# A fused attention and expert kernel: x transposed by its transfer, and the first block in another order

## What is computed

```python
x = x + layernorm(attention(layernorm(x)))
x = x + layernorm(experts(layernorm(x)))

# attention(y): 8 heads of 32, linear, chunks of 64
q, k, v = y @ Wq.T, y @ Wk.T, y @ Wv.T
o = q @ (running sum of k.T @ v) + masked(q @ k.T) @ v
denom = maximum(abs(sum(q * cumsum(k))), 1.0)
o = rmsnorm(o / denom, norm_w) @ Wo
# experts(y): 8 experts of 256, all of them on every row, weighted by a router
out = sum_e w_e * ((silu(y @ Wg[e]) * (y @ Wu[e])) @ Wd[e])
```

## Time and profile before

| | |
|---|---|
| median of 3 runs | 1476.51 us (1476.43 to 1479.62) |
| the profiled execution | 1476.86 us, of which the span 1475.1 us |
| PE, DVE, ACT, POOL busy | 98%, 68%, 43%, 29% of the span |
| from block to block | 89.2 us (transposes of x from 66.8 to 1315.3 us, 14 blocks) |

### The profile page before, as it was taken

How to read it: one execution, slowest core, us unless ns; L and a number is a source line. 1 busy time by engine, 2 the same in 40 slices (tenths; PEclk the granted TensorE clock), 3 DMA queues, 4 the chain that set the end, 5 groups by cost and what they waited for, 6 DMA issues and landing times. The chain is left out here.

```text
span 1475.1 us, 36709 instructions
## 1 busy us (share of the span) xinstructions
PE 1450.9 (98%) x14182; PEld 1263.7 (86%) x14182; DVE 1000.3 (68%) x2397; ACT 629.5 (43%) x1159; POOL 425.6 (29%) x621
## 2 busy tenths in 40 slices
PE   7899999999999999999999999999999999999997
PEld 6688888888888888888888888888888888888886
DVE  6757667586675767667585675767667676675765
ACT  5434534444353443534445353443534345344432
POOL 2402424123241223414134241232413134241230
PEclk9999999999999999999999999999999999999999
DMA  5100000000000000000000000000000000000000
GB/s 173 58 2 16 15 0 14 14 14 14 0 27 1 14 14 14 14 0 14 14 14 14 0 14 14 14 14 0 28 0 14 14 14 14 0 15 16 1 8 22
DMA packets 25344, 24.58 MB, mean 17 GB/s; under 512 B 2016, under 2 KB 25056, under 8 KB 25312
## 3 DMA queue, kind: packets, MB, share of 16 engines
q1 hardware_dynamic: 25312, 24.13, 5.2%
HBM read 15.74 MB, written 8.39 MB: 16 GB/s over the span
## 5 line engine op out<-in xcount | busy, mean ns | idle before, releaser
L1057 DVE TENSOR_TENSOR late<-late,up_ps 128x512 f32<-128x512 f32 x256 | 175.0, 683 | 145.6 <-PE up_ps L455 113.5
L825 ACT ACTIVATE late<-gate_ps 128x512 f32<-128x512 f32 x256 | 152.6, 596 | 278.0 <-PE gate_ps L455 277.2
L455 PE MATMUL down_ps<-w_hi,h_hi 128*128 128x256 f32 x976 | 264.7, 293 | 0.0
L735 ACT ACTIVATE h_hi<-late 128x512 fp32r<-128x512 f32 x256 | 161.2, 630 | 225.1 <-DVE late L1057 225.0
L455 PE MATMUL down_ps<-w_hi,h_lo 128*128 128x256 f32 x976 | 254.2, 282 | 0.0
L1291 POOL TENSOR_TENSOR rms_in<-rms_in,minus_half 128x16 f32<-128x16 f32 x32 | 93.4, 2918 | 489.5 <-DVE rms_in L1005 489.5
L1079 DVE SCALAR_TENSOR_TENSOR late<-down_ps,route,late 128x256 f32<-128x256 f32 x364 | 158.5, 477 | 86.8 <-PE down_ps L455 84.2
L937 DVE TENSOR_TENSOR h_lo<-late,h_hi 128x512 fp32r<-128x512 f32 x256 | 175.6, 686 | 61.0 <-ACT h_hi L735 61.0
L455 PE MATMUL gate_ps<-ft_hi,w_hi 128*128 128x512 f32 x512 | 204.3, 399 | 1.2 <-ACT ft_hi L735 0.8
L455 PE MATMUL gate_ps<-ft_hi,w_lo 128*128 128x512 f32 x512 | 203.0, 397 | 0.0
L455 PE MATMUL up_ps<-ft_hi,w_hi 128*128 128x512 f32 x512 | 199.7, 390 | 0.0
(11 more groups left out here) (175 smaller groups left out, 2381.7 us busy)
## 6 DMA issues: line engine op xcount, KB each, us to landing
xs<-in_x SPq DMA_DIRECT2D x32, 256.0 KB, 2.8
out_rows<-late SPq DMA_DIRECT2D x32, 256.0 KB, 2.2
late<-in_wg SPq DMA_DIRECT2D x7, 256.0 KB, 2.7
late<-in_wu SPq DMA_DIRECT2D x7, 256.0 KB, 4.4
late<-in_wd SPq DMA_DIRECT2D x6, 256.0 KB, 4.1
late<-in_wkv_t SPq DMA_DIRECT2D x1, 512.0 KB, 4.0
x<-in_wd SPq DMA_DIRECT2D x2, 256.0 KB, 5.6
late<-in_wq_t SPq DMA_DIRECT2D x1, 256.0 KB, 4.7
```

The source lines that it names most:

```text
L455: last = nc.tensor.matmul(dst, lhs, rhs, start=n == 0, stop=n == len(terms + low_terms) - 1)
L735: return nc.scalar.activation(dst, src, ACT.Copy)
L825: nc.scalar.activation(h_f[:, m, :], gate_ps[:, :], ACT.Silu).then_inc(silu_ready[0], 1)
L1057: nc.vector.tensor_tensor(h_f[:, m, :], h_f[:, m, :], up_ps[m][:, :], ALU.mult).then_inc(h_ready[0], 1)
```

## The change

First, x transposed. From block 1 on PE no longer transposes. The raw x comes a second time by transfer, element by element, into `x_t`, the free half of `kz`: eight transfers of 128x128 elements a block. SP issues those of block i+1 when block i has split its own, and those of block 1 when the scores of block 0 are done; there they stand behind all weight units. ACT and DVE split `x_t`. The mean is taken out by centred weights: at the start PE forms the column means of the q, k and v weights with a matrix of 1/256 in `rz`, and DVE subtracts them before they are split. The inverse deviation comes in where ACT copies k and v out of PSUM, tile by tile, as a scale; q stays unscaled, and the bound of the denominator is multiplied by x's variance instead, which POOL writes to `var_s` and four small transfers (`place_var`) bring into the layout of the heads (`var_o`). `normalise_x` goes.

Second, block 0. Its PE transposes now go into banks of their own order, its steps stand in another order on all four engines, with other counts of warm-up products, and `x_stats` of block 1 stands behind the first expert's hidden steps on DVE, `x_root` behind `routing` on POOL.

The diff, cut:

```diff
+FIRST_PE = [("xt", 0), ("xt", 1), ("kv", 0), ("kv", 1), ("q", 0), ("su", 0), ("kt", 0), ("su", 1), ("q", 1), ("kt", 1),
+            ("s", 0), ("s", 1), ("o", 0), ("o", 1), ("ot", 0), ("ot", 1), ("wo", 0), ("wo", 1), ("ft", 0), ("ft", 1)]
...
+FIRST_WARM = {("kv", 0): 3, ("kt", 0): 1, ("su", 1): 2, ("s", 1): 1, ("ot", 0): 16, ("ot", 1): 8, ("ft", 0): 27, ("ft", 1): 3}
...
+        x_t = kz[:, :, :, 1, :]
...
+            def load_x_t(row):
+                for t in range(TILES):
+                    p, b = divmod(t, B)
+                    for k in range(KT):
+                        sp.dma_start(x_t[:, k, p, b * P:b * P + P],
+                                     x[b, bass.ds(row + p * P, P), k * P:k * P + P].rearrange("c n -> n c"),
+                                     allow_slow_non_contiguous=True).then_inc(xt_loaded[0], 16)
+
+
+            def place_var(block):
+                reach(sp, var_ready, block, 0)
+                for g in range(HG):
+                    for i in range(2):
+                        sp.dma_start(var_o[C * g:C * g + C, :, i], var_s[C * i:C * i + C, :], allow_slow_non_contiguous=True).then_inc(var_loaded[0], 16)
...
+            reach(sp, att_done, (0, 0), number_of(("s", 1), (0, 0)) + 1)
+            load_x_t(ROWS)
             reach(sp, x1_ready, (0, 0), 2)
             load_x(ROWS)
+            place_var((1, 0))
             with sp.Fori(1, BLOCKS - 1) as i:
+                reach(sp, xt_ready, (i, 0), KT)
+                load_x_t(i * ROWS + ROWS)
                 reach(sp, x1_ready, (i, 0), 2)
                 load_x(i * ROWS + ROWS)
+                place_var((i, 1))
                 store_out((i, -1), i * ROWS - ROWS)
...
-                    else:
-                        k = step[1]
-                        reach(pe, xn_ready, a, TILES)
-                        for t in range(TILES):
-                            last = nc.tensor.transpose(dst[:, t // 2, t % 2 * P:t % 2 * P + P],
-                                                       rows[:, t, k * P:k * P + P], ident[:, :])
...
+            warm(6)
+            for n, (raw, loaded, columns) in enumerate(((wkv_raw, att_w_loaded[1], 2 * HID), (wq_raw, att_w_loaded[0], HID))):
+                pe.wait_ge(loaded, 16)
+                for k in range(KT):
+                    last = nc.tensor.matmul(up_ps[n][:, 0:columns], rz, raw[:, k, :], start=k == 0, stop=k == KT - 1)
+                last.then_inc(mean_done, 1)
...
+                elif kind == "xt":
+                    reach(act, xt_loaded, a, 0)
+                    copy(halves(xt_hi[:, step[1], :]), x_t[:, step[1], :, :]).then_inc(xt_hi_ready[0], 1)
...
+                elif kind == "kv" and not is_first(a):
+
+                    reach(act, rstd_ready[0], a, 2)
+                    for b in range(B):
+                        t = 2 * step[1] + b
+                        last = nc.scalar.activation(k_sb[:, t, :], src[:, b, 0:HID], ACT.Copy, scale=rstd1[:, t:t + 1])
...
-                if more:
-                    normalise_x((a[0], a[1] + 1))
...
+                    else:
+
+                        reach(dve, var_loaded, a, 0)
+                        den_sq, bounded = (flat.rearrange("p b (i j) -> p (b i) j", i=2) for flat in (o_sq[:, :, :, D], den2[:, :, :]))
+                        nc.vector.scalar_tensor_tensor(bounded, den_sq, RMS_EPS,
+                                                       var_o[:, 2 * p:2 * p + 2, :].rearrange("p b i -> p (b i)").unsqueeze(2)
+                                                       .broadcast_to([P, 2 * B, HPG]), ALU.mult, ALU.max)
...
-            x_stats((1, 0))
             low_of_unit(UNITS - 2)
             low_of_unit(UNITS - 1)
             for m in range(MT):
                 hidden(0, m, (0, 0))
                 low_hidden(0, m, (0, 0))
+            x_stats((1, 0))
             first_expert((1, 0), (0, 0), None)
```

More of the change, by code:

```diff
@@ L85 @@
 ]
[L88 to L99, removed]
-             ("ln3_stats", 0), ("ln2_stats", 1), ("unit", 18), ("ln2_add", 1), ("ln3_stats", 1), ("ln3_norm", 0), ("unit", 19),
-             ("ln3_norm", 1), ("ft_out", 0), ("ft_out", 1), ("unit", 20), ("unit", 21)]
@@ L291, in build_program @@
         READ_OUT = {ROUTER: (rz_copied, 1), ROUTER_T: (tanh_ready, 1)}
-        for n in range(KT):
-            READ_OUT["xt", n] = (xt_ready, n + 1)
         for n in range(HG):
@@ L495, in att_step @@
             def att_step(step, a):
+                if step[0] == "xt" and is_first(a):
+                    p = step[1]
+                    pe.wait_ge(xn_ready[0], 2 * p + 2)
+                    for k in range(KT):
+                        for t in range(2):
+                            last = nc.tensor.transpose(att_ps[:, 2 * p + k, t * P:t * P + P], rows[:, 2 * p + t, k * P:k * P + P],
+                                                       ident[:, :])
+                    last.then_inc(xt_done, 1)
                 if step not in PSUM_STEPS:
@@ L704, in _ @@
                 att_step(step, (0, 0))
+            warm(3)
             pe.wait_ge(w_ready, ATT_W + 3)
@@ L743, in ln_apply @@
                 return last
-            def normalise_x(a):
-                for t in range(TILES):
-                    ln_apply(1, 2, a, rows, xs, [t], shift1, rstd1).then_inc(xn_ready[0], 1)
             def normalise_out(p, f):
@@ L757, in att_step @@
                 half = slice(2 * P * step[1], 2 * P * step[1] + 2 * P) if len(step) > 1 else None
-                if kind == "xt":
-                    copy(xt_hi[:, :, half] if is_first(a) else halves(xt_hi[:, step[1], :]), src).then_inc(xt_hi_ready[0], 1)
+                if kind == "xt" and is_first(a):
+                    act.wait_ge(xt_done, step[1] + 1)
+                    copy(xt_hi[:, :, half], att_ps[:, 2 * step[1]:2 * step[1] + 2, 0:2 * P]).then_inc(xt_hi_ready[0], 1)
+                elif kind == "xt":
+                    reach(act, xt_loaded, a, 0)
+                    copy(halves(xt_hi[:, step[1], :]), x_t[:, step[1], :, :]).then_inc(xt_hi_ready[0], 1)
                 elif kind == "q":
                     copy(q_t[:, :, half] if is_first(a) else q_t[:, step[1], :], src).then_inc(q_ready[0], 1)
+                elif kind == "kv" and not is_first(a):
[3 more added lines that the diff above has]
+                        last = nc.scalar.activation(k_sb[:, t, :], src[:, b, 0:HID], ACT.Copy, scale=rstd1[:, t:t + 1])
+                    last.then_inc(k_ready[0], 1)
+                    for b in range(B):
+                        t = 2 * step[1] + b
+                        last = nc.scalar.activation(v_sb[:, t, :, 0:D], src[:, b, HID:2 * HID].rearrange("p (h d) -> p h d", h=H),
+                                                    ACT.Copy, scale=rstd1[:, t:t + 1])
+                    last.then_inc(v_ready[0], 1)
                 elif kind == "kv":
@@ L905, in _ @@
             high(0, 0, (0, 0))
-            normalise_x((1, 0))
             router_tanh((0, 0))
@@ L966, in att_step @@
                     reach(dve, xt_hi_ready, a, k + 1)
-                    low(lo, att_half(step, a), hi).then_inc(xt_ready[0], 1)
+                    low(lo, att_ps[:, 2 * k:2 * k + 2, 0:2 * P] if is_first(a) else x_t[:, k, :, :], hi).then_inc(xt_ready[0], 1)
                 elif kind == "s" and not is_first(a):
```

62 lines of the change are left out of this document (41 added, 21 removed).

## The result

| | before | after |
|---|---|---|
| median | 1476.47 us (4 runs, 1474.71 to 1479.62) | 1792.43 us (4 runs, 1791.13 to 1792.99) |
| ratio after to before | | 1.2138, 95% interval 1.2123 to 1.2153 |
| span of the profiled run | 1475.1 us | 1790.6 us |

The forecast was 1486 us in a range of 1460 to 1530. The sign was right and the size was not: the kernel became 316 us slower, not 10. It is the rival called "the stream is slower than a block", from a cause that the prediction gave only in part.

What follows compares the result with a forecast made beforehand. PE, busy 98% of the span, was taken to bound the kernel: 1476.9 us, minus 14 x 0.79 for transposes removed, plus 20.6 for block 1's stall, gives 1486.4 us; range 1460 to 1530.

Steps and rivals of the forecast that it cites:

- the stream is slower than a block: Blocks wait for x: elements exceed 75 us of room, from 9.2 ns each; 2670 us at 18.6 ns; chance 0.18.
- PE bounds it, and the transposes are worth 0.79 us a block: Steady blocks cost what PE issues; removing eight transposes of x gains 0.79 us in each of 14 blocks.
- 6 ns an element, and the bound of 9.3: Element transfers: 9.3 ns each at most from small packets, 6 ns chosen for overlap, giving 49 us a block.
- the high end of 76: A block's element stream takes 76 us at the upper price, against 49 forecast and 38 at the low end.
- The stream starts 4.0 us into the block: In steady blocks SP issues the next elements after the second xt_lo, 4.0 us in, leaving up to 75 us.
- its own formula: In 14 steady blocks, each loses the time by which its element stream exceeds the room of 75 us.
- The rows behind the stream are the first to be late: Late in steady blocks the rows xs queue behind the elements; PE can bear about 1.5 us of delay there.
- Block 1: 20.6 us: In block 1 PE waits before up(1,1) for elements issued at 37 and landed at 88 us, costing 20.6 us.
- the first block's order gains 2 to 4 us: Block 0's new step order gains 2 to 4 us to its end, vanishing in block 1's wait.
- ACT's four scaled copies, POOL, the variances: nothing: Steady blocks: scaled copies cost ACT 2.1 against 1.2 us, variances under 1 us; nothing on PE.
- The rule of the Trainium skill: Strided transposing copies are 19 times slower than the crossbar's: by estimate 25 us a tile, kernel some 3,360 us.
- The chances: Whole kernel: faster 0.17, same within 0.3% 0.17, slower 0.66; the forecast case itself 0.47.

Runs made afterwards that it cites:

- The two kernels that gave back 9 us each: Changed kernel with one element tile issued ahead of the output store: 1675.43 us; changed kernel with the next rows issued from ACT's queue: 1669.86 us.
- three queues: Changed kernel with rows issued from ACT's queue and output stored from POOL's, leaving SP elements and variances: 1572.28 us; later variants also transpose block 1's x on PE.
- The half stream: Changed kernel with 4 element-by-element tiles a block in place of 8, the other half of x_t keeping old contents: 1486.93 us.
- the other two forms: Changed kernel with elements read in memory order and written to every second element: 2395.2 us; changed kernel with 8-byte pairs, half as many items: 1553.62 us.
- the two kernels without: Kernel before with only the new first-block order: 1476.26 us; changed kernel with PE transposing raw rows and no element transfers: 1480.98 us.
- the kernel with the order alone: Kernel before with the changed kernel's first-block order and warm-up counts, without the two centring steps: 1476.26 us, ratio 1.000.
- the kernel at 1524.25: Changed kernel with rows on ACT's queue, output on POOL's, and block 1's x transposed by PE from raw rows: 1524.25 us, ratio 1.0318.

## Why the prediction failed, step by step

**PE bounds it, and the transposes are worth 0.79 us a block.** Right. 88.2 to 88.3 us block to block where the stream is hidden, against 89.1.

**6 ns an element, and the bound of 9.3.** The term of the sum that was mis-sized. It measured 9.8 ns, 80 us a block in place of 49, outside even the high end of 76. The step that failed is the reading of the earlier trace rows in two places: a share over 100% in a window of 0.1 us was taken as a sign that packets overlap on an engine for good, by a third; and "at most" was written over a figure from 136 packets of another shape. In the stream of elements overlap is short: the share is 125.9% from 46.0 to 46.5 us, at its start, but 87% over 10 us, so that an element takes on average 1.3 ns more than is recorded for it. The second window of the earlier trace rows had a share of 95.9% already, and I counted it as full. The 9.3 ns were within 6% of the truth, and the discount that I chose was the error; but that they were so near is in part luck, since from 6.5 to 6.6 us the same trace has 49 small and 7 larger packets at 233.5%, by the same sum some 69 ns for each small one.

**The stream starts 4.0 us into the block.** Wrong, and not seen at all. The diff shows `store_out` of the last block between place_var and the next load_x_t. In a loop, what stands last in one pass stands ahead of the first in the next; SP reaches it 15.8 us into a block. The room for the stream was thus about 61 us (75 - 14), which decides from 7.5 ns on and not from 9.2. The two kernels that gave back 9 us each show it; the ones with three queues show the converse, that 80 us fit from an early start: ACT no longer waits for x_t in the steady blocks. So the forecast would have been wrong with 9.8 ns alone as well: by its own formula 14 blocks x (80 - 75) is 70 us, under a third of what was lost in them.

**The rows behind the stream are the first to be late.** Right: x_stats waited for xs in all 14 blocks, and x_t for the first time when the rows had another queue. I had not counted that SP is held at its issues for 70 us. I gave PE 1.5 us of patience for rows that come late, and the kernels with the rows on ACT's queue show how little that is: two issues 5 us too late cost 49 us in 14 blocks, clock and all.

**Block 1: 20.6 us.** It was 50.2 of wait. The copies began at 124.63, where I had the landing at 88: 31 us of it are the element's price (80 in place of 49), 6.8 the start (issue at 43.80 in place of 37), and the 1 us that I had for the landing is not seen. Unit 17's low was put at 36 and ended at 43.36, as the second norm_stats ended at 42.76. The first kv began at 15.84 us, at the upper end that I gave (16; my choice was 14), behind a wait of 2.00 us for xt_lo, and the 17 us of work and 1 to 3 of waits behind it were short. That the first block's order gains 2 to 4 us was wrong: the order gives nothing (1.000), and the rest of the changed first block costs 4.2, with 1.5 of it by a lower clock that the prediction did not have.

**ACT's four scaled copies, POOL, the variances: nothing.** Right. The half stream has all of them, and its blocks take 88.2 us. A scaled copy of 256 columns measured 0.47 us (median of 60).

**The rule of the Trainium skill** ("VectorE: DVE Perf Modes", three transpose paths). It gave some 3,360 us by an estimate of 25 us a tile; a tile took 10.0 us, so the measurement decides and the estimate is 2.5 times too dear here. I had left out the page's condition, that the innermost stride of the destination is large; in these transfers the destination's is one element and the source has the stride, and no run has the form that the page speaks of. Its direction was right, and it spoke for the rival of 9 ns and above, as the bound of 9.3 did; I gave that 0.18, and the range left it out.

**The chances** don't quite follow from their parts: these give 0.15 for faster and 0.68 for slower, where 0.17 and 0.66 stand.

**What stays open**: why the elements spread unevenly over the engines in the other two forms; what an item costs from start to start when the spread is another, since 7.0 to 9.8 ns were seen; and what PE's gap under the first stream is. It is seen once in each kernel that has streams, at the same products of block 1's or the next block's attention (3.34 us at 170.24 in after, 2.7 to 6.0 in the others), and not at these products in before or the two kernels without. A gap without a wait isn't bound to a stream, though: in the first block, while weights are loaded, the kernel with the order alone has one of 2.5 us. The times of the instruction transfers speak for late instructions, but that the stream holds them up, and that these are PE's own, is inferred and not tested.

## What to carry to other kernels

Before pricing a new transfer, write down the whole queue that it enters, around the loop's back edge: what must be issued before it, how late in the block that becomes ready, and who stands behind it. The room is what is left between the two, and it was 61 us here and not 75. Where the trace has a price for the nearest small packet, take it from several windows and put the range around it on both sides. And a hidden stream of 80 us for eight transposes of 0.1 us each buys at most 0.85 us a block, so the downside deserved the weight in the range.

## What the runs showed of the hardware

- A transpose by the transfer, 4 bytes an element: 9.8 ns for each element and engine with all 16 at work (9.4 inside a tile), 10.0 us for 128x128, at 7 GB/s. It is the same at half the count. The recorded time is 8.5 ns for an item of 4 bytes and for one of 8.
- SP is held at such issues for about 9.6 us each. From issue to landing each takes 20.7 us (median of 120) at 10 us of flow, so two are under way, and the next waits. A short transfer behind them in program order is not issued for 70 us.
- 256 KB of rows from another queue still go through under a running stream, in 4.5 to 5.2 us in place of 2.8; 1 KB of variances right behind a stream in its own queue took up to 11.1 us in the kernel with three queues, where the median was 1.9.
- How the elements lie on the 16 engines depends on the form of the transfer: 64 partitions written kept under half of their time busy (43.2% from 60.5 to 64.5 us), and a strided destination left most of them idle at the end of each transfer.
- A pause of PE of 18 us costs 2.3 us more behind it, 5 us at 0.54. Behind one of 2.16 us, in the kernel at 1524.25, the clock stood at 0.81 and 0.77 in the two stretches of 4 us from 352 on; its mean from 600 to 1400 us was still 0.99.
- PE stopped for 2.7 to 6.0 us without a wait, once in each of the ten kernels with a stream, and went on 2.7 to 2.9 us after a 16 KB transfer of instructions had begun.
